# A fused attention and expert block on one core: positions read out of PSUM by VectorE, counts and masks summed in one step, expert numbers written by ScalarE, two sends one milestone earlier

## What is computed

```python
logits = xf.astype(jnp.float32) @ w_router.T
gates = jax.nn.softmax(logits, axis=-1)
topk_gates, topk_idx = jax.lax.top_k(gates, TOP_K)
expert_mask = jax.nn.one_hot(topk_idx, N_EXPERTS, dtype=jnp.int32).sum(axis=1)
capacity = math.ceil(N / N_EXPERTS * CAPACITY_FACTOR)
position_in_expert = jnp.cumsum(expert_mask, axis=0) - 1
expert_mask = expert_mask * (position_in_expert < capacity)
keep = jnp.take_along_axis(expert_mask, topk_idx, axis=1) > 0
topk_gates = topk_gates * keep
topk_gates = topk_gates / (topk_gates.sum(axis=-1, keepdims=True) + 1e-06)
```

## Time and profile before

| | |
|---|---|
| time, median of 3 runs | 872.08 us (871.83 to 877.49) |
| the profiled execution | 877.7 us, of which the span is 876.0 us |
| attention pipeline, about | 27 to 564 us of the span |
| last rows sent, about | 564 to 603 us |
| experts, about | 603 to 876 us |
| TensorE busy | 790.7 us, 90% |
| VectorE busy | 596.9 us, 68% |
| ScalarE busy | 490.0 us, 56% |
| GpSimd busy | 474.4 us, 54% |

### The profile page before, as it was taken

One profiled execution on the slowest core, in us unless ns is written; L12 is line 12 of the kernel. 1 busy time (PEld: TensorE's weight loads), 2 busy tenths in 40 slices (PEclk: granted clock), 3 DMA queues, 4 the chain that ended last, 5 costly groups with the idle time before them and its releaser, 6 DMA issues.

```text
span 876.0 us, 24409 instructions
## 1 busy us (share of the span) xinstructions
PE 790.7 (90%) x9388; PEld 649.8 (74%) x9388; DVE 596.9 (68%) x1777; ACT 490.0 (56%) x1001; POOL 474.4 (54%) x591
## 2 busy tenths in 40 slices
PE   5899999999999999999999999622999998899993
PEld 4676776777777777777777776412999998899993
DVE  4666686887877887877877867660667746557652
ACT  5556666665765766756666664231655554454541
POOL 2202345664664764655666645574466656556654
PEclk9999999999999999999999999855999999999997
DMA  5579913323332333222222312224376665676553
GB/s 192 196 223 276 291 14 111 97 87 111 97 84 102 98 89 109 69 91 79 58 79 70 47 53 56 38 78 144 75 164 138 142 157 121 131 150 150 115 96 42
DMA packets 71427, 99.02 MB, mean 113 GB/s; under 512 B 7810, under 2 KB 52866, under 8 KB 71320
## 3 DMA queue, kind: packets, MB, share of 16 engines
q1 hardware_dynamic: 38744, 53.93, 22.6%
q0 software_dynamic: 21760, 31.66, 16.5%
q10 hardware_dynamic: 10816, 11.96, 4.3%
HBM read 46.84 MB, written 63.36 MB: 126 GB/s over the span
## 4 chain that ended last, share of the span: by engine, by line
PE 52%; DVE 13%; issue 12%; POOL 12%; DMA 6%; ACT 3%; POOLq 0%; ACTq 0%; SPq 0%; DVEq 0%
PE PJ L1325 9%; PE SCW L1229 6%; DVE Sm L891 6%; PE SCW L1265 6%; PE SCW L1477 5%; PE MD L1298 5%; POOL out L582 4%; DMA out<-EX,desti 3%; PE SCW L1249 3%; PE MD L1492 3%; PE SCW L1492 3%; PE SCW L1290 2%; PE PJ L1309 2%; PE SCW L1255 2%; PE MD L1239 2%
## 5 line engine op out<-in xcount | busy, mean ns | idle before, releaser
L483 POOL DMA_INDIRECT slot_rows<-Hrow,sloti x128 | 127.6, 997 | 150.9 <-PE SCW L1255 70.3
L891 DVE TENSOR_TENSOR Sm<-SCW,tri 128x1024 f32<-128x1024 f32 x128 | 150.6, 1218 | 57.2 <-PE SCW L1229 55.8
L582 POOL DMA_INDIRECT out<-EX,desti x80 | 127.3, 1592 | 30.3 <-issue 29.8
L1325 PE MATMUL PJ<-hT,w_qkv 128*128 128x512 f32 x384 | 108.5, 419 | 0.3 <-ACT hT L637 0.3
L1325 PEld LDWEIGHTS PJ<-hT,w_qkv 128*128 128x128 f32 x384 | 71.2, 192 | 20.5 <-issue 7.2
L1265 PE MATMUL SCW<-Sm,VA 128*17 128x128 f32 x2048 | 80.6, 275 | 0.0
L1229 PE MATMUL SCW<-QM,KT 32*128 32x256 f32 x1024 | 73.9, 402 | 7.1 <-ACT OTs L767 6.7
L1298 PE MATMUL MD<-w_og,ATs 128*128 128x256 f32 x256 | 73.3, 409 | 0.5 <-ACT ATs L756 0.5
L433 POOL TENSOR_TENSOR idle<-mhalf 128x1 f32<-128x1 f32 x100 | 27.1, 271 | 83.8 <-DVE EX L1164 57.3
L652 ACT ACTIVATE N<-X,nb,rs 128x256 f32<-128x256 f32 x128 | 66.3, 591 | 10.2 <-POOL nb L519 10.2
L648 ACT ACTIVATE EX<-PJ 128x512 f32<-128x512 f32 x64 | 37.9, 592 | 58.6 <-PE PJ L1325 58.6
(11 more groups left out here) (189 smaller groups left out, 1798.0 us busy)
## 6 DMA issues: line engine op xcount, KB each, us to landing
Hrow<-slot_rows SPq DMA_DIRECT2D x32, 516.0 KB
slot_rows<-erow ACTq DMA_DIRECT2D x1, 10400.0 KB, 45.7
X<-x SPq DMA_DIRECT2D x16, 512.0 KB, 4.7
out<-X SPq DMA_DIRECT2D x16, 512.0 KB
Hrow<-mod_rows SPq DMA_DIRECT2D x16, 512.0 KB, 8.1
QT<-slot_rows SPq DMA_DIRECT2D x8, 516.0 KB
slot_rows<-Hrow,sloti POOLq DMA_INDIRECT x128
N<-wd SPq DMA_DIRECT2D x4, 512.0 KB
```

Of the source, the lines that this page charges most:

```text
L483: pool.indirect_dma_start(xe, bass.IndirectOffsetOnAxis(sloti[:, 1 - gp, k, t:t + 1], 0), Hrow[:, 1 - gp, t, :], None, bounds_check=SLOTS ...
L582: pool.indirect_dma_start(out, bass.IndirectOffsetOnAxis(desti[s % 2][:, a:a + 1], 0), Ys[s % 2][:, a, :], None, bounds_check=TOK - 1, oob ...
L891: dve.tensor_tensor(o.rearrange("p c (k w) -> p c k w", k=2), SCW[:, 2 * pair:2 * pair + 2, :].rearrange("p k (c w) -> p c k w", c=DC), tr ...
L1325: last = mm(PJ[m % 2][:], w_qkv[:, wp, cc, m * P:(m + 1) * P], hT[:, hp, cc, :], start=(cc + i == 0), stop=(cc == DC - 1 and i == len(SPLI ...
```

## The change

`take(pos, ...)` on ScalarE is gone: VectorE's two steps that need the positions read them in PSUM, as the first gap of the q=3 slot, where `place_expert` stood. What waited for the copy (`taken`) now waits for these two steps (`route` at 15). `msum` and the addition to `macc` are one `tensor_reduce` over five slices of a new tile `masks`: the four tiles' masks and the running count at one end; the result goes to the other end, so the two ends alternate by group. `route` counts 28 steps. ScalarE writes the expert number as the third of its small activations of the q=2 slot. On GpSimd the last two sends of a group each move a milestone ahead: `send_row(3, 0)` from `knt_full` to `on_full`, `send_row(3, 1)` from `state_full`, behind the first pair of powers, to `knt_full`, ahead of them. On ScalarE the two roundings (`stage1_hi`) of the q=0 slot stand behind the eviction of `OTs` instead of ahead of it.

```diff
-NR = 29
+NR = 28
...
-        mask = sb("mask", [P, GT, E], BF16)
-        msum = sb("msum", [P, E])
-        macc = sb("macc", [P, E], BF16)
+        masks = sb("masks", [P, GT + 2, E], BF16)
+        mask, macc = masks[:, 1:GT + 1, :], [masks[:, 0, :], masks[:, GT + 1, :]]
...
                 if paced and q == 2:
                     pool.wait_ge(sc_full[1], 2 * T + 2)
                     send_row(2, 1)
+                    pool.wait_ge(on_full, T)
+                    send_row(3, 0)
                     pool.wait_ge(knt_full, T + 1)
-                    send_row(3, 0)
+                    send_row(3, 1)
                 if q == 2 and group_ok(gn - 1) and gn != GROUPS:
                     deviations(rs2, vp2, nm2, nb2, vpe2, pow2, rstd2, G)
-                if paced and q == 2:
-                    pool.wait_ge(state_full, T + 1)
-                    send_row(3, 1)
...
-                if q == 3 and group_ok(gn - 2):
-                    take(pos, pos_ps, pos_full, G)
...
                 if stage1 and q == 0:
                     stage1_transposed(it, G, 1, bcol)
-                    stage1_hi(G, 0)
-                    stage1_hi(G, 1)
...
                     act.activation(OTs[:].rearrange("p (c b) i -> p b c i", c=DC), OB, ACT.Copy).then_inc(ot_done, 1)
+                if stage1 and q == 0:
+                    stage1_hi(G, 0)
+                    stage1_hi(G, 1)
...
                     act.activation(e12[:, 1, :], m2[:], ACT.Exp).then_inc(gexp, 1)
+                    if g >= 2:
+                        act.wait_ge(sent[gp], 128 * (g // 2))
+                    act.activation(Hrow[:, gp, :, D + 3:D + 4], rk[:, 0, :].unsqueeze(2), ACT.Copy,
+                                   scale=-1.0, bias=float(E)).then_inc(gexp, 1)
...
-                before_step = (13, 17, 20, 22, 23, 25, 26, 27, 28, 29)
+                before_step = (13, 15, 18, 20, 22, 24, 25, 26, 27)
                 if k == 0:
-                    dve.wait_ge(taken, 2 * g + 2)
-                    dve.wait_ge(gexp, 2 * g + 2)
+                    dve.wait_ge(pos_full, g + 1)
...
-                    done(dve.tensor_scalar(drop[:], pos[:], float(CAP), BIG, ALU.is_ge, ALU.mult))
-                    done(dve.tensor_tensor(pbase[:], pos[:], base[:].unsqueeze(1).to_broadcast([P, GT, E]), ALU.add))
-                    done(dve.tensor_reduce(msum[:], mask[:].rearrange("p t e -> p e t"), AX_X, ALU.add))
+                    done(dve.tensor_scalar(drop[:], pos_ps, float(CAP), BIG, ALU.is_ge, ALU.mult))
+                    done(dve.tensor_tensor(pbase[:], pos_ps, base[:].unsqueeze(1).to_broadcast([P, GT, E]), ALU.add))
+                elif k == 1:
+
+                    with nc.allow_low_precision(reason="whole numbers up to 64 are exact"):
+                        done(dve.tensor_reduce(macc[1 - g % 2], masks[:, g % 2:g % 2 + GT + 1, :].rearrange("p t e -> p e t"),
+                                               AX_X, ALU.add))
+                    dve.wait_ge(gexp, 3 * g + 3)
...
-                    done(dve.tensor_tensor(macc[:], macc[:], msum[:], ALU.add))
...
                     if tile_ok(n - 1):
-                        normalise_heads(T, lambda: place_expert(gp), lambda: None)
...
+                        normalise_heads(T, between, lambda: None)
...
                         if group_ok(gn - 2):
-                            pe.wait_ge(taken, 2 * (G - 2) + 2)
+                            pe.wait_ge(route, NR * (G - 2) + 15)
                         stage1_v(G, 1)
```

More of the change, by code:

```diff
@@ L404, in _ @@
             pool.memset(mhalf[:], -0.5).then_inc(consts, 1)
-            pool.memset(macc[:], 0.0).then_inc(consts, 1)
+            pool.memset(macc[0], 0.0).then_inc(consts, 1)
             pool.memset(e12[:], 1.0).then_inc(consts, 1)
@@ L952, in choose @@
                 if k == 0:
-                    dve.wait_ge(taken, 2 * g + 1)
+                    dve.wait_ge(taken, g + 1)
                 else:
@@ L981, in choose @@
                 elif k == 12:
[L982 removed]
+                    done(dve.tensor_tensor(mask, oh[:, 0], oh[:, 1], ALU.add))
             def place(it, g, pg, gn, k):
[L986 removed]
+                before_step = (13, 15, 18, 20, 22, 24, 25, 26, 27)
                 if k == 0:
[L988 to L989 removed]
+                    dve.wait_ge(pos_full, g + 1)
                 elif k <= 8:
@@ L1024, in place @@
                                            esum[:].unsqueeze(1).to_broadcast([P, 2, GT]), ALU.mult))
-            def place_expert(pg):
-                row = Hrow[:, pg].rearrange("p t r -> p r t")
-                dve.tensor_scalar(row[:, D + 3:D + 4, :], rk[:, 0:1, :], -1.0, float(E), ALU.mult, ALU.add)
             def slot_(it, j, n):
@@ L1346, in h2_transposes @@
                 if gn >= 3:
-                    pe.wait_ge(taken, 2 * (G - 2))
+                    pe.wait_ge(route, NR * (G - 3) + 15)
                 if group_ok(gn):
@@ L1389, in positions @@
                 all_ = pos_ps
-                mm(all_, before[:], mask[:], start=True, stop=True, skip_group_check=True)
+                mm(all_, before[:], mask, start=True, stop=True, skip_group_check=True)
                 for t in range(GT - 1):
@@ L1393, in positions @@
                        start=False, stop=True, skip_group_check=True)
-                mm(all_, ones[:], macc[:].unsqueeze(1).to_broadcast([P, GT, E]), start=False, stop=True,
+                mm(all_, ones[:], macc[g % 2].unsqueeze(1).to_broadcast([P, GT, E]), start=False, stop=True,
                    skip_group_check=True).then_inc(pos_full, 1)
@@ L1438, in slot_ @@
                         if group_ok(gn - 2):
-                            pe.wait_ge(taken, 2 * (G - 2) + 1)
+                            pe.wait_ge(taken, G - 2 + 1)
                         stage1_qk(G, 1)
```

11 lines of the change are left out of this document (2 added, 9 removed).

## The result

The changed kernel takes 866.04 us in the median of 20 runs (863.32 to 874.15), the kernel before, run beside it, 874.74 (869.41 to 880.29): a ratio of 0.991, 95% interval 0.989 to 0.993. That is 8.7 us, 0.9%, faster than before by just under the 1% that I had drawn as the line. The interval leaves no doubt that it is faster. The profiled execution has a span of 863.6 us against 876.0.

The account below looks back on a forecast made before the run. TensorE, busy 90% of the 876.0 us span, was taken to bound the kernel, so only its waits could pay. Gains of 6.2 + 0.3 + 1.9 + 1.2 = 9.6 us off the 872.08 us median gave 862.5 us, range 858 to 869.

Parts of the forecast that it names:

- The sum: Whole kernel: gains of 6.2, 0.3, 1.9 and 1.2 us, 9.6 us together, for 862.5 us.
- faster by over 1%: Whole kernel: a gain over about 8.7 us, a time below 863.4 us; chance 0.55.
- one of the prediction's own signs of being wrong: Last group's row transposes, line 1355: the sum is wrong if they start less than 8 us earlier.
- A second sign: Last group's line 1355: TensorE was to stand idle under 0.8 us ahead of it.
- Step 1, heads: Starts of q=0 slots: VectorE 1.2 us a group shorter brings eleven heads to 2.61 us; 6.2 us, plus 0.3 in the sixteenth group.
- Steps 2 and 3: PSUM bank held longer by the positions, and ScalarE's swapped small copies: nothing lost or gained in time.
- Step 4, sends: GpSimd's last two sends earlier: `modulate` 1.0 us sooner, 1.9 us gained in the last group, bounds 0 and 2.6.
- Step 5, `OTs`: q=0 slots: eviction ahead of the roundings removes TensorE's waits, partly given back at line 1325; 1.2 us, between 0 and 3.9.
- The rival "slower": 14 groups: GpSimd's subtraction later by 1.3 us each makes the kernel 9.8 us slower, 881.9 us; chance 0.03.

Follow-up runs that it names:

- P: Edit label: positions read from PSUM, counts and masks in one step, expert number on ScalarE; alone on the kernel before: 871.6 us, ratio 0.995.
- S: Edit label: a group's last two sends moved earlier; alone on the kernel before: 885.0 us, ratio 1.012 on chip A.
- R: Edit label: copy `OTs` put ahead of the roundings; together with S on the kernel before, without P: 868.6 us, ratio 0.992.
- place_alone: The kernel before with P only, sends and roundings as before, on chip B: 871.6 us, ratio 0.995.
- before_again: The kernel before, unchanged, run and profiled again on chip A: 876.7 us, ratio 1.001.
- after_look: The changed kernel (P, S and R) again, one run on chip C: 881.1 us.

## Why the prediction was right, and where it was not

- *The sum.* 9.6 us forecast, 8.7 measured; 866.04 lies in the range of 858 to 869. That the number is so near is partly luck. Gains that I had too small stood against a loss that I had not seen, and the kernel was timed where the moved sends do no further harm: on chip C the same kernel took 881.1 us in its one run, outside the range. The forecast of "faster by over 1%" as the likeliest was wrong by a hair. And one of the prediction's own signs of being wrong came true: the last group's line 1355 was to start at least 8 us earlier and starts 6.5 earlier (556.77 for 563.26). A second sign, idling under 0.8 us there, failed with 1.41.
- *Step 1, heads: right in size, wrong in whose work it is.* 6.2 us forecast for the eleven heads, 6.4 measured; 0.3 and 0.4 for the sixteenth. But the step said that VectorE's 1.2 us a group do it. P alone leaves 0.14 us in each head, and S with R, without P, reaches the same 2.63. The step's own evidence said that `macc` is long because GpSimd's modulation runs; the conclusion should have been that whoever moves the modulation cures it as well.
- *Steps 2 and 3: right* as far as can be seen: no wait for the bank and none for the expert number appears.
- *Step 4, sends.* "I take `modulate` 1.0 us earlier; that covers the waits at 1355 inside part 1" left the steady groups no cost, and that failed. I followed what the send leaves (the second powers, `modulate`) and not what it now stands ahead of: the first power. On chips without late copies this started 0.10 us ahead of the feature map (`place_alone`, 1.09 us long) and now starts 0.02 ahead of it, and is 0.5 us longer. Price 5.8 us. The profile of before could not show how near the two were: there the late `OTs` had pushed the feature map to 0.69 behind the power. The way out was sized at 1.9 us, and from tile 60 on 4.0 were saved: 1.2 between tiles 60 and 63 (0.4 of it the sixteenth group's head), 1.5 from there to the start of line 1348, and 1.4 behind it. Of the 2.0 worked out for `modulate`, 0.5 is missing since the step took the norms to stay where they were, and the send pushed their power, too. The 1.4 had not been counted, and is the clock, which one of two profiles of the kernel before also kept.
- *Step 5, `OTs`.* 1.2 forecast, 3.2 measured, in slots that no run takes apart on a chip without late copies. Behind the first group it is 1.8: 0.13 to 0.18 in an odd group, 0.05 to 0.11 in an even one. The mechanism is as described but the give-back was too small: 0.44 us in the q=1 slot, where the working had 0.21 of 0.55. The step's own halving made up for it. The first group had not been looked at: its two slots went from 17.3 to 15.8 us. All eight profiles with a rounding moved have 15.7 to 15.8 there, and five of the six without it 17.2 to 17.3, so the edit seems to do most of this; the sixth, `before_again`, has 15.8 without it, and why is open.
- *The rival "slower"* had the wrong mechanism. There is a slower outcome, 881 us for the changed kernel on one chip (C); two variants with the same sends took 885.0 and 881.7 on A, and one of them 882.3 on C. It comes with two sends back to back, which no step had as a risk, and not from the subtraction. I gave "slower" 0.03.
- *What bounds this result.* The profile of before has the late `OTs` (1.3 us), that of after has not, so they may compare two kinds of chip. For the kernel before this is worth little: it took 874.9 to 875.9 on all four. Kernels that ran on one chip can be compared without this. No run takes both sends out of the changed kernel on a chip without late copies, so what S is worth there as a whole is added up from slots.
- *Open.* Whether the chip decides, or something that was set when the programs were loaded: all profiles of one set agree, but no chip came up twice. What stops TensorE and ScalarE was not found either; the transfers run alike in both kinds of profile. In the five half microseconds from the start of tile 26's second half of products, the DMA share is 0.25, 1.00, 0.18, 0.60 and 0.74 in after (from 247.87) and 0.21, 0.97, 0.22, 0.58 and 0.77 in `after_look` (from 252.20).

## What to carry to other kernels

When an instruction is moved in a queue, price what it is now ahead of as carefully as what it leaves behind, down to the tenths by which the next one meets another engine's long operation. Where a short step is stretched by a neighbour, look for the edit that moves the neighbour before shortening the step. And be wary of two indirect sends from GpSimd back to back beside work on the critical path: on one chip the slots with both took 9.72 us, and 8.28 with the second send moved away. Time a kernel on more than one chip before you believe a per cent.

## What the hardware showed that was not expected

- A power on GpSimd of 4 elements a partition with both inputs in SBUF takes 1.01 to 1.07 us with nothing beside it, and 1.61 when VectorE's feature map begins 0.03 us behind it; it takes 1.09 when that begins 0.10 behind it (`place_alone`) and 1.04 when 0.29 behind it. The Trainium skill, SBUF — State Buffer, "Who interferes with whom", has such a pair contend, with the first to issue taking the port and the other blocked. Here the first to start was the one that got longer, by 0.57 us, and VectorE's operation stayed at 0.71 us, so this trace does not agree with the order in that rule, if the start in the trace is what the page means by issue. In four of the 48 cases within 0.05 us the power was no longer than 1.06.
- On two of four chips, beside an indirect send that runs from 0.06 us ahead of the products' second half to 0.92 behind it, ScalarE's `OTs` begins at 1.24 to 1.33 instead of 0.70; where two sends stand 0.3 us apart, `ATs` begins about 1.65 us late and TensorE stops between matmuls that wait for nothing. On the other two chips the same instructions at the same offsets do nothing of the kind. A kernel whose timing leaves room there, like the one before, takes the same time on all four.
